# Last stage of a two-layer graph kernel: a quad of graphs passes in six steps instead of seven, with new places for four pieces of work

## The reference

```
    y = (y - mg) / jnp.sqrt(vg + EPS) * gg + beg       # end of layer 0
    y = _leaky(y)
    out = jnp.concatenate([x, y], axis=2) @ Wt.T + bt
    ...
    x = x + _L0_gnn_ref(h, adj, ...)
    h = jnp.maximum(_layernorm(x, axis=-1), 0.0)
    x = x + _L1_gnn_ref(h, adj, ...)

def _L1_gnn_ref(inputs, adj, W, a):
    h = jnp.einsum('bnf,fo->bno', inputs, W)
    attn_self = h @ a[:F_OUT]
    attn_neigh = h @ a[F_OUT:]
    dense = attn_self + jnp.swapaxes(attn_neigh, 1, 2)
    dense = jnp.where(dense >= 0, dense, ALPHA * dense)
    attention = jnp.where(adj > 0, dense, NEG_INF)
    attention = jax.nn.softmax(attention, axis=1)
    h_prime = jnp.einsum('bnm,bmo->bno', attention, h)
    return jax.nn.elu(h_prime)
```

## Time and profile before

| | value |
|---|---|
| median of 3 runs | 1139.58 us (1136.91 to 1140.4) |
| the profiled execution, its own time | 1137.62 us |
| its span in the trace | 1135.6 us |
| busy over the whole span | PE 93%, DVE 92%, ACT 88%, POOL 50% |
| last stage (first `outputs` matmul to the end of the last `elu`) | 1039.40 to 1132.80 us |
| in that stage, 1040 to 1133: busy | PE 83.2, ACT 83.0, DVE 81.8, POOL 25.7 of 93 us |

### The profile page before, as it was taken

One profiled execution on the slowest core, in us unless ns is written; L12 is line 12 of the kernel. 1 busy time (PEld: TensorE's weight loads), 2 busy tenths in 40 slices (PEclk: granted clock), 3 DMA queues, 4 the chain that ended last, 5 costly groups with the idle time before them and its releaser, 6 DMA issues.

```text
span 1135.6 us, 17511 instructions
## 1 busy us (share of the span) xinstructions
PE 1052.9 (93%) x6390; PEld 462.9 (41%) x6390; DVE 1041.5 (92%) x1397; ACT 1001.5 (88%) x1268; POOL 563.0 (50%) x315
## 2 busy tenths in 40 slices
PE   3999999999999999999999989899999999978997
PEld 1333333333333333343333444233333333357786
DVE  5999999999999999999999985899999999948897
ACT  4888999999999999999999978999999999934897
POOL 6586678777776877776686700211121231201330
PEclk9999999999999999999999989999999999989999
DMA  6444444444444444444444487999998999860012
GB/s 181 167 158 158 161 164 177 177 167 167 195 167 169 175 177 158 171 190 167 177 186 177 176 325 255 321 351 337 332 353 322 348 330 337 307 176 10 20 57 75
DMA packets 99059, 233.30 MB, mean 205 GB/s; under 512 B 9120, under 2 KB 46464, under 8 KB 98976
## 3 DMA queue, kind: packets, MB, share of 16 engines
q1 hardware_dynamic: 86704, 219.97, 52.6%
q0 software_dynamic: 2240, 7.34, 1.8%
q10 hardware_dynamic: 10032, 4.89, 1.7%
HBM read 124.43 MB, written 107.74 MB: 204 GB/s over the span
## 4 chain that ended last, share of the span: by engine, by line
PE 46%; DVE 28%; ACT 13%; issue 8%; ACTq 2%; DMA 1%; POOL 1%; DVEq 0%; POOLq 0%
PE psum L780 18%; DVE store L294 11%; PE psum L790 10%; PE psum L794 7%; ACT store L665 5%; DVE plain_st L1093 4%; ACT store L584 4%; PE psum L893 3%; DVE store L1125 2%; PE psum L770 1%; PE psum L868 1%; PE psum L752 1%; ACTq L669 1%; DVE bst L1280 1%; DMA fold<-fold_in 1%
## 5 line engine op out<-in xcount | busy, mean ns | idle before, releaser
L294 POOL TENSOR_TENSOR store<-h_ext 128x2048 f32<-128x2048 f32 (+1 forms) x96 | 386.6, 4029 | 120.0 <-PE psum L780 116.1
L780 PE MATMUL psum<-store,w1tt_sb 128*64 128x512 f32 x1792 | 421.4, 598 | 19.4 <-ACT store L584 19.1
L294 DVE TENSOR_TENSOR store<-psum,h_ext 128x2048 f32<-128x2048 f32 x160 | 363.7, 2273 | 0.0
L584 ACT ACTIVATE store<-store 128x2048 f32<-128x2048 f32 x160 | 305.1, 1931 | 10.9 <-DVE store L294 7.7
L665 ACT ACTIVATE store<-store,st 128x1024 f32<-128x1024 f32 x192 | 227.9, 1240 | 0.0
L780 PEld LDWEIGHTS psum<-store,w1tt_sb 128*64 128x64 f32 x1792 | 122.2, 136 | 254.5 <-issue 226.4
L790 PE MATMUL psum<-store,w_twice 128*64 128x512 f32 x768 | 200.8, 600 | 6.9 <-DVE early L1058 3.5
L294 DVE TENSOR_TENSOR store<-h_ext 128x2048 f32<-128x2048 f32 x64 | 146.3, 2285 | 17.8 <-PE psum L780 17.8
L1093 DVE BATCH_NORM_STATS2 plain_st<-store 128x6 f32<-128x512 f32 x256 | 160.4, 676 | 0.0
L794 PE MATMUL psum<-early 128*64 128x512 bf16 x1152 | 158.2, 380 | 0.0
L893 PE MATMUL psum<-store,w_rows 128*32 128x512 f32 x1024 | 135.0, 609 | 8.8 <-ACT store L665 8.8
(11 more groups left out here) (161 smaller groups left out, 1091.3 us busy)
## 6 DMA issues: line engine op xcount, KB each, us to landing
kept_products<-store SPq DMA_DIRECT2D x192, 512.0 KB, 2.8
store<-kept_products SPq DMA_DIRECT2D x192, 512.0 KB, 5.8
early<-score_skew POOLq DMA_DIRECT2D x14, 384.0 KB, 6.5
early<-adj SPq DMA_DIRECT2D x16, 256.0 KB, 3.6
early<-adj_t SPq DMA_DIRECT2D x16, 256.0 KB, 3.6
store<-x ACTq DMA_DIRECT2D x16, 256.0 KB, 5.3
out<-early SPq DMA_DIRECT2D x16, 256.0 KB, 2.3
score_skew<-early POOLq DMA_DIRECT2D x14, 128.0 KB, 6.1
```

Of the source, the lines that this page charges most:

```text
L294: return engine.tensor_tensor(t[:, :, 0:steps, :], nodes.unsqueeze(2).broadcast_to([C, 2, steps, N]), windows(h_ext[:, 2 * c, :], STEP * m ...
L584: nc.scalar.activation(t, t, ACT.Abs).then_inc(abs_ready, 1)
L780: last = nc.tensor.matmul(t[MID * g:MID * g + MID, b, :], w1tt_sb[:, 0:MID], diff[slot][:, g, b * BANK:b * BANK + BANK], start=True, stop= ...
```

## The change

The lags of `dense`, `masked`, `weigh`, `attend` and `elu` each fall by one, so the stage has 22 steps instead of 23. `dense_leaky` keeps its lag of 4 and gets a name of its own for it (`LOW2`), as `values` does (`VALUES`, from 5 to 4). Inside a step the orders become:

- PE: `turn2`, `outputs`, `values`, `attend`, `dense` (before: `turn2`, `dense`, `outputs`, `values`, `attend`).
- ACT: `elu_exp`, `turn_out2`, `dense_leaky`, `normal`, `exps2` (before: `elu_exp`, `normal`, `turn_out2`, `dense_leaky`, `exps2`).
- DVE: `scales2`, `weigh`, `residual`, `masked`, `variance`, `elu` (before: `scales2`, `residual`, `variance`, `masked`, `weigh`, `elu`).

No instruction is added or removed.

```diff
-        H2, TURN2, DENSE, MASKED, WEIGH, ATTEND, LAST = 2, 3, 4, 5, 6, 6, 7
+        H2, TURN2, DENSE, VALUES, LOW2, MASKED, WEIGH, ATTEND, LAST = 2, 3, 3, 4, 4, 4, 5, 5, 6
         STEPS = NQ + LAST
...
             for t in range(STEPS):
-                for lag, do in ((LAST, elu_exp), (H2, normal), (TURN2, turn_out2), (DENSE, dense_leaky),
-                                (MASKED, exps2)):
+                for lag, do in ((LAST, elu_exp), (TURN2, turn_out2), (LOW2, dense_leaky), (H2, normal), (MASKED, exps2)):
...
-                for lag, do in ((TURN2, turn2), (DENSE, dense), (-1, outputs), (MASKED, values), (ATTEND, attend)):
+                for lag, do in ((TURN2, turn2), (-1, outputs), (VALUES, values), (ATTEND, attend), (DENSE, dense)):
...
             for t in range(STEPS):
                 if t % 2 == 0 and 2 <= t <= NQ:
                     scales2(variance_of(t - 1))
+                if 0 <= t - WEIGH < NQ:
+                    weigh(t - WEIGH)
                 if t < NQ:
                     residual(t)
                 if t == 1:
                     scales2(0)
+                if 0 <= t - MASKED < NQ:
+                    masked(t - MASKED)
                 if t == 0 or t % 2 == 1 and t < NQ:
                     variance(variance_of(t))
...
-                for lag, do in ((MASKED, masked), (WEIGH, weigh), (LAST, elu)):
-                    if 0 <= t - lag < NQ:
-                        do(t - lag)
+                if 0 <= t - LAST < NQ:
+                    elu(t - LAST)
```

## The result

The changed kernel is slower: 1146.9 us, median of 7 runs (1142.93 to 1150.96), against 1136.91 us for the kernel before on the same chips (7 runs). The ratio is 1.0087 (1.007 to 1.0104), so 8.0 to 11.8 us more. (The 1139.58 us ahead of the prediction is the median of the first three of these seven runs of the kernel before.) In the two profiled executions the times are 1137.62 and 1147.0, the spans 1135.6 and 1145.0. The last stage, from the first matmul of `outputs` to the end of the last `elu`, grew from 93.4 us (1039.40 to 1132.80) to 102.4 us (1039.80 to 1142.19): 9.0 of the 9.4 us between these two executions. From here on "the stage" is this length, since it is free of what varies ahead of it.

A forecast was written before the change was run, and what follows sets the result against it. The last stage was taken as bound by VectorE's work and waits. New waits 3.6 + 2.6 + 2.7 + 4.4 = 13.3 less 6.5 removed give +6.8 us on 1139.58, so 1146.4 us; own range 1143.5 to 1149.5, whole 1141.5 to 1150.5.

The forecast's parts named there:

- the drain: End of the stage, walked from `weigh`(11) in step 16: VectorE's waits sum to 4.4 us against 3.5 before.
- VectorE bounds the stage, and its waits are the change: Last stage: as long as VectorE's work and waits; the work stays, new waits are 13.3 us, removed ones 6.5.
- Wait A: VectorE's `scales2` waits for POOL's power: 0.52 us at steps 8, 10, 12, 14, 16 (2.6 in all), 1.85 at step 6.
- rival 3: Even steps: `elu` holds POOL's power up by up to 0.68 us, five times; +3.4 us, 1149.8 us, chance 0.07.
- Wait B: VectorE's `weigh` waits for the same quad's exponentials: 0.45 us ahead of odd steps 7 to 17 (2.7), 1.78 ahead of step 5.
- The pair of steps: Middle of the stage, two steps of VectorE: 11.2 us instead of 10.20.
- rival 4: TensorE's clock falls again after its waits, and the drain's matmuls double at 1.2 GHz: +4.5 us, 1150.9 us, chance 0.06.
- The filling: First steps of the stage: new waits 1.78 + 1.85 = 3.6 us, removed 3.0 from `residual` of steps 6 and 7.
- A and B were not hidden: Judges the rival that both waits are hidden after all: 5.3 goes from the sum, +1.5, 1141.1 us, chance 0.11.
- the shorter pipeline: Rival: the pipeline ends a step earlier and each step keeps its 5.10 us on average; 1134.5 us, chance 0.06.

The follow-up runs named there:

- The experiment on the kernel before: Eight matmuls that nobody reads added on TensorE ahead of `turn2` of step 5, against the kernel before: stage 91.8 us, ratio 0.9991 (0.9981 to 1.000).

## Why the prediction was right, point by point

The forecast was +6.8 us (1146.4 us), the measured ratio gives +9.9 (8.0 to 11.8), the stage +9.0. The mechanism was right, and one term of the sum, the drain, was 2.2 us too small. That the measured median, 1146.9, lies only 0.5 from 1146.4 is luck: the base of the forecast, 1139.58, was the median of three runs and lies 2.7 above that of all seven, which made up for most of what the rise was short of.

- *VectorE bounds the stage, and its waits are the change.* Right: its waits rose by 8.4 us of idle time, 21 of them instead of 10, each of which hides about 0.08 more, and the stage rose by 9.0.
- *Wait A, `scales2` for POOL:* said 0.52 from step 8 on and 1.85 in step 6; measured 0.53 (1096.59 to 1097.12) and, as idle time, 1.75. POOL's power took 1.66 beside `elu`, so rival 3 did not come. The Trainium skill, page "SBUF — State Buffer", section "Who interferes with whom", describes the lock as one that the engine that starts first holds for its whole instruction. Between the power and VectorE these rows show none; the last section has rows of another GpSimd instruction that look like it, for about a third of that instruction.
- *Wait B, `weigh` for the exponentials:* said 0.45 and 1.78; measured 0.48, and 1.72 as idle time. The hand-over from `masked` to `exps2`, which no row had shown, gives 0.97 from the start of `masked` to the first exponential (1088.45 to 1089.42), so the 0.03 that I chose was right.
- *The pair of steps:* 11.2 said, 11.19 measured. From `residual` of step 4 to the last one it is 61.0 us (1053.29 to 1114.31) against 52.2, 8.8 more; 8.7 was said. (3.8 of it is work that the shorter lags bring ahead of the last `residual`: one `masked`, two `weigh`, one `elu`.)
- *The drain* is the term that was too small. (Its waits before the change were five and not the seven that I counted, which is 3.4 instead of 3.5.) From the last `residual` to the end I said about 26 us; it is 27.9 (1114.31 to 1142.19). These are the waits there, VectorE of the changed kernel, from step 17 on:

```profile
1123.10 0.18 DVE L1313 RECIPROCAL soft<-soft 128x4 f32<-128x4 f32 x1 [0.44 <-ACT store L725]
...
1126.70 0.29 DVE L1306 CUSTOM_DVE_ANT_0 store<-store,early 128x128 f32<-128x128 f32 x1 [2.70 <-ACT store L720]
...
1129.77 0.18 DVE L1313 RECIPROCAL soft<-soft 128x4 f32<-128x4 f32 x1 [0.80 <-ACT store L725]
...
1140.77 0.69 DVE L1324 SCALAR_TENSOR_TENSOR early<-psum,h_nat 128x512 f32<-128x512 f32 x1 [1.06 <-ACT store L733]
1141.50 0.69 DVE L1327 SCALAR_TENSOR_TENSOR early<-store,early 128x512 f32<-128x512 f32 x1
```

The waits of `weigh`(12) and `weigh`(13) came within 0.1 of the walk. `masked`(13) waited 2.70 for a walked 1.17, and the last `elu` 1.06 for 0.64. Both stand behind matmuls at the low clock: that is rival 4, which I had set beside the forecast at 0.06 and +4.5 us, and of which 2.2 came true, on top of the forecast. Filling the pauses took these 2.2 us off and left +6.8, the sum of the forecast, so this is shown. What failed is the step in which I walked the drain at the full clock, though rival 4 itself said that TensorE would wait most in the drain. The clock of the earlier trace rows had followed this row of the kernel before, a wait of 2.69 us for `turn_out2`, which stood behind `normal` on ScalarE:

```profile
1055.26 0.63 PE L970 MATMUL psum<-ident,store 128*128 128x128 f32 x4 [2.69 <-ACT h_ext L714]
```

- *The filling:* new waits 3.6, removed 3.0 by the list, as said. But the reason that I gave, a `residual` that comes late, is only half of it. The change puts `turn_out2` ahead of `normal` on ScalarE, and the same `turn2` then waits 0.17 us, and the clock stays at 1.00:

```profile
1055.11 0.65 PE L969 MATMUL psum<-ident,store 128*128 128x128 f32 x4 [0.17 <-ACT store L707]
```

The two kernels of the experiments that keep ScalarE's old order without filling the pause have a long pause at about this place (2.70 us ahead of this `turn2` with seven steps, 2.31 ahead of a `dense` with six) and the low clock behind it (0.50 and 0.55); in the filling of those with the new order there is neither. The experiment on the kernel before shows that the clock alone was worth 1.6 us of the stage. A change of the order on ScalarE had thus removed a fall of TensorE's clock.
- *The other rivals:* A and B were not hidden, and the shorter pipeline did not win the 5.1 us of a step: with six steps and without A and B the stage is as long as before (93.4 us both).

## What to carry to other kernels

Taking a step out of a pipeline over several engines pays only if, on each engine, enough other work still stands between giving a piece of work away and needing it back; count that distance, in both directions, against the round trip through the other engines, before anything else. Here the round trips were 1.97 and 2.64 us and the work left in between 1.45 and 2.19, and moving one job of 1.62 us to another place in the list undid the loss. It is a condition and no promise: with these waits gone, six steps took as long as seven, since VectorE's work was the same. And walk the ends of the pipeline with the clock that TensorE will have after its pauses there.

## What was not expected of the hardware

- A VectorE instruction with two inputs from SBUF is held up when it starts shortly behind a GpSimd mask instruction (L517, 128x512, from uint8). In the kernel with `scales2` behind `weigh`, the mask starts 0.22 us ahead of `scales2` in steps 8 to 14, and `scales2` takes 0.41 or 0.42 for 0.16. With `residual` first, the mask starts 0.02 ahead of `scales2` in step 6, which takes 0.61, and 0.36 to 0.38 ahead of the first instruction of `masked` in steps 8, 10 and 12, which takes 0.39 or 0.40 for 0.28. In all of these the held instruction goes on about 0.48 behind the start of the mask, whose record lasts 1.50. What starts 0.49 behind it is not held (the second `elu` instruction in the kernel before), nor is one with a single input from SBUF: in the changed kernel the reciprocal starts 0.03 and the multiplication of `weigh`, whose other input is in PSUM, 0.23 behind a mask, and both keep their 0.17 and 0.69. No run moved the mask, so the cause is read from these coincidences and not shown by an experiment.
- TensorE's clock fell behind a pause of 1.86 us between bursts of matmuls in the drain, stayed at the lower level for about 3 us, and stayed up when 1.46 us of this pause and 0.81 of the one in step 15 were filled. The length of one pause doesn't decide it: behind the 1.78 us ahead of the first `turn2` (1047.60 in the changed kernel) the clock stayed at 1.00 in the changed kernel and the kernel before, and with ScalarE's old order it fell in the drain behind one of 1.64.
- It did not fall in the middle of the changed kernel, where TensorE paused 0.58 or 0.59 us in steps 8, 10 and 12 and 0.95 in step 14.
